# Low halves of queries and keys on another engine, reciprocals in PSUM, shorter routing, and a new order of the projections in a transformer block with routed experts

## The reference

```
q = (LN(x) wq' + bq) / 4;  k = ctx wk' + bk;  v = ctx wv' + bv
x = x + tanh(g0) * (softmax(causal(q k')) v wo' + bo)
xn = LN(LN(x)) * gamma + beta
probs = softmax(xn Wr');  top 2 experts of 8
rank of each (token, choice) in its expert; kept while rank < 640
y = W3 (silu(g) * u) of the expert's rows
x = x + tanh(g1) * sum of prob * y
```

## Time and profile before

| | |
|---|---|
| Median of 3 runs | 534.14 us (533.56 to 534.17) |
| The profiled execution | 534.19 us |
| Its span, first to last instruction | 532.3 us |
| Mean granted PE clock | 0.973 of full speed |
| Busy: PE, DVE, ACT, POOL | 90%, 68%, 56%, 39% of the span |
| Attention rounds | from 19 us to about 203 us |
| Tail and scatters | to about 234 us |
| Experts | to 532.3 us |

### The profile page before, as it was taken

The page is one execution under the profiler, slowest core; times in us unless marked ns, Lnnn a source line. Parts: engine busy times, 40 slices in busy tenths (PEclk is TensorE's granted clock), DMA queues, the critical chain, the costliest instruction groups (busy, mean ns, idle before and its releaser), DMA issues.

```text
span 532.3 us, 10749 instructions
## 1 busy us (share of the span) xinstructions
PE 479.7 (90%) x3551; PEld 444.7 (84%) x3551; DVE 360.8 (68%) x854; ACT 298.9 (56%) x757; POOL 208.9 (39%) x272
## 2 busy tenths in 40 slices
PE   5699999899999877369998999999999999999991
PEld 4588887777877666269998999999999999999991
DVE  6867888988888997547876574485843768544240
ACT  3689878677778764416664564373723747423230
POOL 8636776787787566510212012203032030311202
PEclk9999999999999997779999999999999999999996
DMA  8868432314142611153677362347451474201111
GB/s 269 209 140 250 78 41 72 75 57 81 42 80 55 205 42 53 58 175 118 234 184 219 78 226 34 60 129 193 132 144 20 130 188 131 31 4 17 13 19 20
DMA packets 41649, 57.33 MB, mean 108 GB/s; under 512 B 3721, under 2 KB 38576, under 8 KB 39552
## 3 DMA queue, kind: packets, MB, share of 16 engines
q1 hardware_dynamic: 35168, 48.62, 31.7%
q0 software_dynamic: 6144, 8.07, 9.1%
q10 hardware_dynamic: 288, 0.00, 0.0%
HBM read 36.24 MB, written 16.72 MB: 99 GB/s over the span
## 4 chain that ended last, share of the span: by engine, by line
PE 55%; DVE 3%; issue 2%; POOL 1%; DMA 0%; ACT 0%; POOLq 0%; DVEq 0%
PE bank L1438 17%; PE bank L1440 17%; PE bank L1439 17%; PE bank L1432 2%; PE bank L1361 1%; PE bank L1304 1%; POOL expert_rows L484 0%; DMA expert_rows<-xr,slotu 0%; DVE pT L929 0%; PE bank L1290 0%; POOL out_tokens L546 0%; DVE nm L924 0%; PE bank L1231 0%; PE bank L1238 0%; DVE osum L938 0%
## 5 line engine op out<-in xcount | busy, mean ns | idle before, releaser
L546 POOL DMA_INDIRECT out_tokens<-ysc,rows x32 | 49.6, 1550 | 245.6 <-DVE ysc L1142 238.9
L1438 PE MATMUL bank<-bXh,wh 128*128 128x384 f32 (+1 forms) x384 | 122.1, 318 | 2.9 <-issue 2.6
L1440 PE MATMUL bank<-bXh,wl 128*128 128x384 f32 (+1 forms) x384 | 121.8, 317 | 0.0
L1439 PE MATMUL bank<-bXl,wh 128*128 128x384 f32 (+1 forms) x384 | 121.8, 317 | 0.0
L749 ACT ACTIVATE sil<-bank 128x384 f32<-128x384 f32 (+1 forms) x96 | 43.7, 456 | 128.4 <-PE bank L1440 127.2
L1121 DVE TENSOR_TENSOR hF<-sil,bank 128x384 f32<-128x384 f32 (+1 forms) x96 | 48.9, 510 | 77.9 <-ACT sil L749 71.3
L633 ACT ACTIVATE p<-bank,nm 128x128 f32<-128x128 f32 x256 | 73.6, 387 | 14.7 <-DVE nm L924 14.7
L1438 PEld LDWEIGHTS bank<-bXh,wh 128*128 128x128 f32 x384 | 72.7, 189 | 3.3 <-issue 3.3
L1438 PE MATMUL bank<-wh,hH 128*128 128x256 f32 x256 | 73.8, 288 | 0.3 <-DVE ysc L1142 0.3
L1439 PEld LDWEIGHTS bank<-bXl,wh 128*128 128x128 f32 x384 | 72.7, 189 | 0.0
L1440 PEld LDWEIGHTS bank<-bXh,wl 128*128 128x128 f32 x384 | 72.6, 189 | 0.0
(11 more groups left out here) (146 smaller groups left out, 878.8 us busy)
## 6 DMA issues: line engine op xcount, KB each, us to landing
stage<-in_w12T SPq DMA_DIRECT2D x16, 1024.0 KB
stage<-in_w3T SPq DMA_DIRECT2D x8, 1024.0 KB
expert_rows<-padrow SPq DMA_DIRECT2D x8, 662.5 KB, 7.9
rows<-expert_rows SPq DMA_DIRECT2D x7, 662.5 KB, 4.4
kM<-k SPq DMA_DIRECT2D x64, 64.0 KB, 2.4
cT<-in_ctxT SPq DMA_DIRECT2D x8, 256.0 KB, 3.1
out_tokens<-x_all SPq DMA_DIRECT2D x8, 256.0 KB, 2.3
x_all<-in_x SPq DMA_DIRECT2D x2, 640.0 KB, 8.5
```

What stands on the lines that cost most here:

```text
L546: pool.indirect_dma_start(out=out, out_offset=bass.IndirectOffsetOnAxis(rows[par][:, c, D + E:ROW].bitcast(U32), 0), in_=ysc[par][:, c, :] ...
L1438: nc.tensor.matmul(out_ap, ah, bh, start=start, stop=False)
L1439: nc.tensor.matmul(out_ap, ah, bl, start=False, stop=False)
L1440: return nc.tensor.matmul(out_ap, al, bh, start=False, stop=stop)
```

## The change

ScalarE rounds both projections directly from PSUM into the high halves (two operations each instead of three; the factor of the queries moves to the copy of the transposed inputs). VectorE makes the low halves, from PSUM, two operations each, in groups 1 and 3. `qT` and `kT` go. `orec` lies in the free columns of the bank that it is made from. The expert probabilities are no longer stored; one operation makes the gate columns from the exponentials and the inverse sum. The ranks are counted by TensorE from the stored members of all earlier sequences, with the expert's first slot included, so that three small VectorE operations of the slots go. On TensorE weighing stands ahead of the projections in each group; keys move from group 2 to group 0, the transposed inputs from 0 to 1, the queries from 4 to 2, the values from 6 to 4, and the ranks behind the group's other work. GpSimd makes the third part of the values in the round before. At the start ScalarE zeroes one part of `kM[0]` that VectorE zeroed. The loops over the rounds are written out on all five engines.

```diff
-        orec = sb(pa, "orec", [P, 8], F32)
+        orec = [O[i][:, 8 * VW:8 * VW + 8] for i in range(2)]
-                sp.wait_ge(pool_kl, n + 1)
+                sp.wait_ge(dve_kl, n + 1)
@@ GpSimd, body
                 if cur:
-                    values_third(n, par)
                     residual(n, par, prev1)
-                if nxt:
-                    keys_low(n + 1)
+                if nxt2:
+                    normalize_inputs(n + 2)
...
                 if nxt:
-                    queries_low(n + 1, 1 - par)
+                    values_rest(n + 1, 1 - par)
...
                 if nxt:
-                    values_rest(n + 1, 1 - par)
+                    values_third(n + 1, 1 - par)
                 if prev2 and cur:
                     token_numbers(n - 2, par)
                     dispatch(n - 2, par)
@@ ScalarE
-            def queries(n, par, bank, prev1):
+            def queries(n, par, bank):
                 act.wait_ge(pe_q, n + 1)
                 for t in range(DC):
-                    act.activation(qT[:, t, :], bank[:, t * SB * T:(t + 1) * SB * T], ACT.Identity,
-                                   bias=bq4[:, t:t + 1], scale=HD ** -0.5).then_inc(act_q32, 1)
-                act.wait_ge(act_q32, DC * (n + 1))
-                act.activation(q2[par][:, 0, :, :], qT[:, :, :], ACT.Copy).then_inc(act_q, 1)
+                    act.activation(q2[par][:, 0, t, :], bank[:, t * SB * T:(t + 1) * SB * T], ACT.Identity, bias=bq4[:, t:t + 1])\
+                       .then_inc(act_qh, 1)
@@ ScalarE, body: each group now copies the probabilities, then the exponentials, then
+                    if g == 0 and nxt:
+                        keys(n + 1, Xp)
+                    elif g == 1 and nxt:
+                        input_columns(n + 1)
+                    elif g == 2 and nxt:
+                        queries(n + 1, 1 - par, Xp)
+                    elif g == 4 and nxt:
+                        values(n + 1, Xp)
+                    elif g == 5 and nxt:
+                        values1(n + 1, 1 - par)
+                    elif g == 7 and nxt:
+                        values2(n + 1, 1 - par)
                     if g == 0 and prev1:
                         output_columns(SB * (n - 1), Xo)
+                    elif g == 2 and prev2:
                         x2_columns(n - 2, Xo)
+                    elif g == 4 and prev1:
                         output_columns(SB * (n - 1) + 1, Xo)
+                        if prev2:
+                            exps_of_logits(n - 2)
@@ VectorE
             def gate_columns(m, mpar):
-                dve.tensor_scalar(xr[mpar][:, :, D:D + E], prob[:, :, :], tg[:, 1:2], None, ALU.mult).then_inc(dve_wp, 1)
+                dve.scalar_tensor_tensor(xr[mpar][:, :, D:D + E], lex[:, :, :], tg[:, 1:2], lrc[:, :].unsqueeze(2).to_broadcast([P, SB, E]),
+                                         ALU.mult, ALU.mult).then_inc(dve_wp, 1)
...
-                dve.tensor_scalar(late[:, :, :], rk, float(CAP), LATE, ALU.is_ge, ALU.mult).then_inc(dve_rk, 1)
-                dve.tensor_tensor(slot0[:, :, :], rk, ebase[:, :].unsqueeze(1).to_broadcast([P, SB, E]), ALU.add).then_inc(dve_rk, 1)
-                dve.tensor_reduce(seen_add[:, :], member[:, :, :].rearrange("p j e -> p e j"), AX_X, ALU.add).then_inc(dve_rk, 1)
+                dve.tensor_tensor(late[:, :, :], rk, limit[:, :].unsqueeze(1).to_broadcast([P, SB, E]), ALU.is_ge).then_inc(dve_rk, 1)
...
-                dve.tensor_tensor(slot[:, :, :], slot0[:, :, :], late[:, :, :], ALU.add).then_inc(dve_rk, 1)
-                dve.tensor_tensor(seen[:, :], seen[:, :], seen_add[:, :], ALU.add)
+                dve.scalar_tensor_tensor(slot[:, :, :], late[:, :, :], LATE, rk, ALU.mult, ALU.add).then_inc(dve_rk, 1)
...
+            def keys_low(n, bank):
+                dve.wait_ge(act_kh, DC * (n + 1))
+                for t in range(DC):
+                    ins = dve.scalar_tensor_tensor(k2[:, 1, t, :], bank[:, t * SB * T:(t + 1) * SB * T], bqkv[:, 1, t:t + 1],
+                                                   k2[:, 0, t, :].bitcast(F32), ALU.add, ALU.subtract)
+                ins.then_inc(dve_kl, 1)
...
                     if cur:
                         largest(G, g)
+                    if g == 1 and nxt:
+                        keys_low(n + 1, Xp)
+                    elif g == 3 and nxt:
+                        queries_low(n + 1, 1 - par, Xp)
@@ TensorE
             def input_columns(n, first, second):
...
-                    pe.wait_ge(act_vf, n)
+                    pe.wait_ge(dve_kl, n + 1)
...
             def ranks(m, bank):
+                nc.tensor.matmul(rk, onesb[:, :], ebase[:, :].unsqueeze(1).to_broadcast([P, SB, E]), start=True, stop=False)
+                for j in range(first):
+                    nc.tensor.matmul(rk, onesb[:, :], member[:, j, :].unsqueeze(1).to_broadcast([P, SB, E]), start=False, stop=False)
                 pe.wait_ge(dve_mem, m + 1)
...
@@ TensorE, body
                     if (cur and g >= 2) or (prev1 and g < 2):
                         prob_columns(G - 2, g % 2, not prev1 and g < 4)
+                    if cur and g >= 3:
+                        weigh_values(G - 3, g - 3, n, par, not prev1 and g < 7)
+                    elif prev1 and g < 3:
+                        weigh_values(G - 3, NG + g - 3, n - 1, 1 - par, False)
                     if nxt:
-                        if g == 2:
+                        if g == 0:
                             keys(n + 1, 1 - par, Xp, use)
+                        elif g == 1:
+                            input_columns(n + 1, False, not prev1)
+                        elif g == 2:
+                            queries(n + 1, Xp)
                         elif g == 4:
-                            queries(n + 1, Xp)
-                        elif g == 6:
-                            pe.wait_ge(act_q32, DC * (n + 2))
+                            pe.wait_ge(dve_ql, n + 2)
                             values(n + 1, 1 - par, Xp)
...
-            with pe.Fori(2, NSB // 2 - 1) as i:
+            for i in range(2, NSB // 2 - 1):
...
-            nc.tensor.matmul(Xo[:, 0:E], onesb[:, :], seen[:, :], start=True, stop=True).then_inc(pe_cnt, 1)
+            for j in range(SEQS):
+                ins = nc.tensor.matmul(Xo[:, 0:E], onesb[:, :], member[:, j, :], start=(j == 0), stop=(j == SEQS - 1))
```

More of the change, by code:

```diff
@@ L128, in gated_block @@
         lrc = sb(pa, "lrc", [P, SB], F32)
-        prob = sb(pa, "prob", [P, SB, E], F32)
         top8 = sb(pa, "top8", [P, SB, 8], F32)
@@ L132, in gated_block @@
         pick = sb(pa, "pick", [P, K, SB, E], F32)
-        member = sb(pa, "member", [P, SB, E], BF16)
-        seen = sb(pa, "seen", [P, E], BF16)
-        seen_add = sb(pa, "seen_add", [P, E], F32)
+        member = sb(pa, "member", [P, SEQS, E], BF16)
         late = sb(pa, "late", [P, SB, E], F32)
-        slot0 = sb(pa, "slot0", [P, SB, E], F32)
         slot = sb(pa, "slot", [P, SB, E], F32)
@@ L208, in gated_block @@
         xv = x_all[:, :].rearrange("p (i d) -> p i d", d=D)
-        R_CHAIN = 4
+        R_CHAIN = 3
         C_CHAIN = 3
-        R_SLOT = 5
+        R_SLOT = 3
         PIECES = 12
@@ L290, in _ @@
             turn(2, 0)
-            with sp.Fori(1, NSB // 2 - 1) as i:
+            for i in range(1, NSB // 2 - 1):
                 turn(2 * i + 1, 1)
@@ L402, in _ @@
             pool.memset(onesb[:, :], 1.0).then_inc(const_ok, 1)
-            pool.memset(seen[:, :], 0.0).then_inc(const_ok, 1)
             for v3 in V3:
@@ L672, in _ @@
             act.wait_ge(ld_b, 16)
-            keys(0, K0, False)
+            act.wait_ge(ident_ok, 1)
+            act.activation(kM[0][:, 1, :, :].rearrange("p h (a t) -> p (h a) t", t=P),
+                           ident32[:, :].unsqueeze(1).to_broadcast([P, 2 * H, P]), ACT.Copy, scale=0.0).then_inc(km_zero[0], 1)
+            keys(0, K0)
             input_columns(0)
@@ L677, in _ @@
             act.wait_ge(bias_ok, 1)
-            queries(0, 0, Q0, False)
+            queries(0, 0, Q0)
             act.activation(kM[1][:, 1, :, :].rearrange("p h (a t) -> p (h a) t", t=P),
@@ L683, in _ @@
             body(1, 1, True, False, True, True)
-            with act.Fori(1, NSB // 2 - 1) as i:
+            for i in range(1, NSB // 2 - 1):
                 body(2 * i, 0, True, True, True, True)
@@ L858, in invert_sum @@
                 dve.reciprocal(lrc[:, :], lse[:, :]).then_inc(dve_r, 1)
-            def expert_probs(m):
-                dve.wait_ge(dve_r, R_CHAIN * m + 3)
-                dve.tensor_tensor(prob[:, :, :], lex[:, :, :], lrc[:, :].unsqueeze(2).to_broadcast([P, SB, E]), ALU.mult).then_inc(dve_r, 1)
             def sort_experts(m):
@@ L939, in heads_out @@
                    .then_inc(dve_os, 1)
-                dve.reciprocal(orec[:, :], ob[:, :, 3 * HD]).then_inc(dve_rec, 1)
+                dve.reciprocal(orec[k % 2], ob[:, :, 3 * HD]).then_inc(dve_rec, 1)
                 dve.wait_ge(dve_os, kk + 1)
```

(15 more changed lines are left out.)

117 lines of the change are left out of this document (43 added, 74 removed).

## The result

The changed kernel takes 545.97 us (545.48 to 548.06, four runs), the kernel before 534.06 beside it: a ratio of 1.0232, interval 1.0205 to 1.026. It is slower, by 11.9 us where 5.85 were forecast. The profiled execution is the slowest of the four: 548.06 us, with a span of 546.4 against 532.3. Its extra 14.1 us are what the trace can place. Each ratio in this document leaves out the executions in a slower state, three in all, among them two of 803 and 1676 us.

What follows compares the result with a forecast made beforehand. TensorE bounds rounds 1 to 6, VectorE round 7. New waits +21.2 us, old waits gone -10.6, round 7 -3.8, tail -0.95: net +5.85 on 534.15 gives 540.0 us, range 530.5 to 545.5.

Steps and rivals of the forecast that it cites:

- Group 1, +6.6: TensorE waits 1.1 us for VectorE's low keys in group 1, in every one of rounds 1 to 6: +6.6 us.
- Group 4, +3.1: In group 4 TensorE waits for VectorE's low halves: +0.35 us in rounds 2 to 6, +1.35 in round 1.
- Round ends, +10.0: Weighing in group 0 of the next round waits 2.0 us for VectorE's low halves, after rounds 2 to 6: +10.0.
- my 21.9: TensorE's work in a routed round (rounds 2 to 6) of the kernel before, small gaps included: 21.9 us.
- Start and round 0, -0.65 + 1.1: Start net -0.65 us: first exponentials earlier, but round 1's keys behind them; round 0's new waits +0.35 and +0.75.
- Rival E: Waits in the rounds bring TensorE's clock to its lower level for part of each: 550 us or more; chance 0.03.
- Round 7, -3.8, and tail, -0.95: Round 7, VectorE-bound, loses 3.8 of 21.60 us; the tail loses 0.95 through slots and probabilities of rounds 5 and 6.
- -2.9 for one long `oN`: In round 7 one `oN` of 3.20 us falls to 0.29 with its factor in PSUM: -2.9 us.
- The slots' -0.55: VectorE's slots per routed round go from 1.29 to 0.75 us with three of seven operations gone: -0.55 us.
- rival C: `gate_columns`, both inputs in SBUF, stretches as `prob` did, 0.87 us in six rounds: 545.2 us; chance 0.10, shared with another rival.
- The experts ..., which it does not touch: The expert stage, after the attention rounds up to about 203 us, was taken as untouched by the change.
- Loops written out: nothing: Rounds 3 to 6 last 24.0 to 24.7 us inside or outside the loops, so writing them out changes nothing.

## Why the prediction was right or wrong

*Direction, and the mechanism of the rounds: right.* POOL's wait went, PE's waits for the low keys and the low probabilities came in the groups that were named, and the loss of rounds 1 to 6 is in them. That of round 0 and of the experts is not.

*Group 1, +6.6:* measured 1.02 us six times, 6.1. Right.

*Group 4, +3.1:* too high. The wait was 1.16 in round 1 (forecast 1.35), but in rounds 2 to 6 only 0.26, 0.17 and three times about 0.14 instead of 0.35: 2.0 in all.

*Round ends, +10.0:* the wait is 0.21 in group 7 and 0.98 in group 0, 1.2 instead of 2.0. The round still came out within 0.1 us of the forecast (25.29 and 25.4), because PE's busy time grew from 22.3 to 23.0, which I had set at nothing (0.08 on each projection that stands behind a weighing, the ranks 0.27 instead of 0.1), and my 21.9 for its work had been a little low to begin with. Errors of opposite sign cancel.

*Start and round 0, -0.65 + 1.1:* the step that failed first. I had seen that the keys of round 1 follow the first exponentials, and took 2 us of it against the earlier start; I did not ask how long PE stands idle there (3.46 us) and what that does to its clock. By its terms and 1.3 us for the projection that moved ahead of the cut, the scores of group 1 in round 1 were due at 42.8; they came at 45.0. The low clock is 1.3 to 1.5 of these 2.2. It is in part luck: three traces with this wait (3.46 us) have it, one with 3.14 hasn't, and two with the order of before have it without the wait. Rival E had the clock only in the routed rounds.

*Round 7, -3.8, and tail, -0.95:* measured -3.1 together: round 7 took 19.70 us, 1.9 less and not under 19 as I had said, the tail 1.2 less. The -2.9 for one long `oN` was mis-sized: alone on the kernel before, the edit brings 0.8 to the experts, and nothing from round 7 to the first of the last scatters. A stretch in which DVE is busy 20.45 of 21.60 us is not one in which each of its microseconds is on the path. The slots' -0.55 failed by operation: `pslot` has two SBUF inputs and fell under GpSimd's work. That is rival C's mechanism at another instruction (`gate_columns` took 0.23), and the slots in PSUM show that its price was about nothing.

*"The experts ..., which it does not touch", and "Loops written out: nothing":* the step that put the result outside the range. The loops are nothing, as forecast. The experts' instructions are untouched, but 68 matmuls ahead of them moved the program, and its branch behind expert 0 stops PE: 4.85 us in the profiled execution, 3.05 of it the stop and the rest the low clock behind it. The same number of matmuls on the kernel before shows it alone: a stop there, and 4.8 us in the median. I had named the sequential prefetch and applied it only to the loops.

*The sum.* +10.6, -4.75 and 0 were forecast for the three stages; +12.4, -3.1 and +4.85 were measured. The other three executions were about 2 us shorter than the profiled one; where is not recorded. With 4.85 for the experts the forecast would have been 544.9.

## What to carry to other kernels

A stage that a change doesn't touch is not exempt: when the program ahead of it grows, a taken branch behind can gain or lose a stop (here of 2.5 to 4.7 us), so compare the stops on "issue" first. Tiny work belongs ahead of a dependent wait only where the next thing would wait anyway: the weighing was free in group 1 and cost about 6 us elsewhere. And a gain on an engine that is nearly full is to be followed to where it lands: an operation of 3.2 us cut to 0.3 in round 7 moved nothing there.

## What was not expected of the hardware

The clock's fall isn't told by the length of a stop alone. In the experts it fell to its lower level behind stops of 3.05 us both times, but behind 3.01 with the weighing moved it did not, nor behind 2.61 in the kernel before; behind 2.62 in the one with the reciprocals moved it did (0.72 from 289.91 to 295.91). In round 0 it fell behind waits of 3.46 and 3.47, not behind 3.14, and in two kernels with the order of before behind one of 1.46. A fall costs 1.3 to 1.9 us, with the weighing behind everywhere nearly 3.

Contention goes by which of the two begins first. GpSimd works beside `pslot` in both kernels. Before, in round 2:

```profile
84.69 0.19 DVE L914 TENSOR_TENSOR pslot<-pick,slot 128x32 f32<-128x32 f32 x1
...
84.71 0.77 POOL L470 TENSOR_TENSOR xr<-xr,beb 128x256 f32<-128x256 f32 x1
```

After:

```profile
92.62 0.73 POOL L454 TENSOR_TENSOR xr<-xr,gab 128x256 f32<-128x256 f32 x1
...
92.66 0.73 DVE L883 TENSOR_TENSOR pslot<-pick,slot 128x32 f32<-128x32 f32 x1
```

Where `pslot` began 0.02 us ahead of GpSimd's operation it took 0.19, as in six rounds before; where it began 0.04 behind, six times in the changed kernel, it ended with that operation, at 93.39 and 93.35. Operands and size are the same. So a shift of 0.06 us between two engines made 0.54 of it. Before, the operation on `slot` ahead of it (L909, two SBUF inputs, 0.57) had ended with GpSimd's previous one; its successor reads PSUM and is not held up, so `pslot` meets the operation instead.

Small matmuls of 8 columns went out every 28 ns (156 in 4.32 us, 68 in 1.96), but not always: at the start of the same wait 13 of them took 5.9 us.
